# First mixture of a two-layer decoder: token weights multiplied into the up product's operand by GpSimd, eight experts' results summed in one bank

## The chip, the cores and the metric

The kernel is one program on one core of a Trainium2 chip. The time is device time in microseconds, the median of several runs. A core has TensorE (PE: matrix products, with PEld for its weight loads), VectorE (DVE), ScalarE (ACT), GpSimd (POOL) and the queue engine SyncE (SP), which here only issues transfers. Each engine works through its own instructions in order; they wait for each other by semaphores.

## The reference

Four batches of 512 tokens of 128 features go through two layers of self attention, cross attention and a mixture of experts. Only the first mixture, on 2048 tokens with 8 experts, matters here:

```python
hidden = x.reshape(-1, H)
routing_weights = jax.nn.softmax(hidden @ gate_w.T, axis=-1)
topk_weights, topk_indices = jax.lax.top_k(routing_weights, 2)
topk_weights = topk_weights / (jnp.sum(topk_weights, axis=-1, keepdims=True) + EPS)
...
routed = routed / (jnp.sum(routed, axis=-1, keepdims=True) + EPS)
...
gate_up = jnp.einsum('th,ehq->teq', hidden, gate_up_proj)
gate, up = jnp.split(gate_up, 2, axis=-1)
expert_outputs = jnp.einsum('teq,eqh->teh', jax.nn.silu(gate) * up, down_proj)
out = jnp.sum(expert_outputs * routed[:, :, None], axis=1)
```

`x` in this formula is the layer norm of the residual rows, and `out` is added to them. `routed` holds a token's weight for each expert, zero for six of eight.

## The kernel before

The first stage of the program (`stage_front`) holds the first layer. Its end, 400 to 510 us of the trace, is the mixture, written as 32 turns: turn `t` is expert `t % 8` of batch `t // 8`. The order of the work on each engine is written out by hand: a loop over `t` on each engine, in which `if t == ...` lines put the rest of the work (what is left of cross attention, layer norms, routing, the layer norm `lq` for the next stage) between the turns.

All experts are computed for all tokens. In a turn TensorE does `gate_up(t)`: a gate and an up product of a whole batch, 512 tokens, into a bank each (L553, L554). Then it does `down_of(t - 1)`, the down product of the turn before, as four products of 128 tokens (L568). ScalarE takes the gate through SiLU (L1009, `silu_of`). VectorE multiplies that by the up result (L836, `hidden`). Both products of `gate_up` read the transposed, normalized rows of the batch in `g.XT`. The down result of each expert lies in one of two banks, tokens on the partitions. VectorE multiplies it by the tokens' weights and adds it to the residual rows `g.X` in four instructions, one for each 128 tokens (L847, `add(t - 1)`, at the end of the turn after):

```python
for i in range(SB):
    n = SB * b + i
    x = g.X[:, n, :]
    last = dve.scalar_tensor_tensor(out=x, in0=down[k][:, i, :], scalar=rt.route[:, e, n:n + 1],
                                    in1=x, op0=ALU.mult, op1=ALU.add)
```

The routing of a batch runs through these steps: TensorE's `route_of` (L545), then on VectorE `rt.shift`, with ScalarE an exponential (L1248), on VectorE `rt.softmax`, `rt.first`, `rt.second` and `rt.weigh`, some 25 short instructions (L1253 to L1290) of which each waits for the one before. The last raises `rt.done`. The rows for it come from a layer norm: `ln2` has statistics on VectorE (L115, L118), the inverse root on GpSimd (L124, L126), the normalization on VectorE (L132), transposes on TensorE (`rows_turn2`, of `ln` `rows_turn`, L159) and a copy on ScalarE (L166). `ln` and `lq` have the same steps. `cross_of`, `cross_add` (L775), `y_of`, `residual` (L749), `logits_of` and `soften` belong to attention and cross attention of batches 2 and 3, which end inside the mixture. `last_pair_head` and `last_pair_tail` (L822 on) are the last heads of the self attention.

## Time and profile before

| | us |
|---|---|
| median of 3 runs | 1030.67 |
| lowest and highest run | 1028.32, 1035.21 |
| profiled execution, first to last instruction (span) | 1028.4 |
| TensorE busy in it | 925.0 |
| VectorE busy in it | 761.6 |
| ScalarE busy in it | 624.5 |
| GpSimd busy in it | 510.8 |

The profiled execution's own time is its span; the page gives no other. Busy times are sums of instruction times; TensorE's instructions overlap in its pipeline, so what one of them costs is read from the start of it to the start of the next. All rows below name lines of the kernel before. A 32-bit product appears as two instructions in the trace.

### The profile page before, as it was taken

Reading aid. Unit: us, or ns where it says so; the run is one execution under the profiler, and the core shown is the slowest. Engines: PE = TensorE matmul, PEld = TensorE weight load, DVE = VectorE, ACT = ScalarE, POOL = GpSimd, SP = SyncE. Lnnn points to the kernel's source line nnn. Section 1 sums busy time; section 2 is a strip of 40 time slices with the busy share of each in tenths; the row PEclk is TensorE's granted clock in tenths of the full one; section 3 lists DMA queues with packets and bytes.
Section 4 is the critical chain, followed back from the end, with each engine's and each line's share of the span. In section 5 each row is a group of like instructions: output and inputs, shape, how many; then the busy total and the mean of one; then the engine's idle time right before and its main releaser. Section 6 shows DMA issues by size and latency. Waiting matters only on the chain. (4 is left out here: it accounts for less than half of the span.)

```text
span 1028.4 us, 20270 instructions
## 1 busy us (share of the span) xinstructions
PE 925.0 (90%) x6146; PEld 480.8 (47%) x6146; DVE 761.6 (74%) x1656; ACT 624.5 (61%) x1500; POOL 510.8 (50%) x847
## 2 busy tenths in 40 slices
PE   3999999999999997899889999999999997888296
PEld 1222222222332334565455555555555564567296
DVE  7799899889999976889745666666656665676464
ACT  4388888888888883233266665665566652354164
POOL 6366666776554462100144454455445443775544
PEclk8599999999999999999999999999999997696599
DMA  4099920000000000000060000000000000000240
GB/s 103 1 237 245 245 60 1 2 1 2 2 1 0 0 1 1 1 1 1 8 206 6 15 9 7 8 13 5 8 5 13 0 2 1 0 2 16 89 122 19
DMA packets 50684, 37.49 MB, mean 36 GB/s; under 512 B 15737, under 2 KB 48677, under 8 KB 50608
## 3 DMA queue, kind: packets, MB, share of 16 engines
q1 hardware_dynamic: 48864, 32.83, 13.4%
q0 software_dynamic: 1744, 3.72, 1.1%
q8 instruction: 39, 0.64, 0.3%
q14 instruction: 37, 0.30, 0.1%
HBM read 15.54 MB, written 21.45 MB: 36 GB/s over the span
## 5 line engine op out<-in xcount | busy, mean ns | idle before, releaser
L725 DVE TENSOR_REDUCE a_nmax<-a_rows 128x2 f32<-128x1024 f32 x256 | 299.7, 1218 | 26.5 <-PE a_rows L439 23.6
L979 ACT ACTIVATE a_probs<-a_turned 128x512 f32<-128x512 f32 x512 | 270.0, 605 | 48.2 <-PE a_turned L465 46.9
L1451 POOL TENSOR_TENSOR a_prob<-a_prob,a_rinv 128x256 f32<-128x256 f32 (+3 forms) x128 | 159.4, 1253 | 163.9 <-DVE a_rinv L1647 163.6
L1640 DVE TENSOR_REDUCE a_nmax<-a_score 128x2 f32<-128x256 f32 (+3 forms) x128 | 105.6, 825 | 116.5 <-PE a_score L1497 112.2
L1594 ACT ACTIVATE a_prob<-a_score,a_nmax 128x128 f32<-128x128 f32 (+3 forms) x256 | 132.6, 523 | 81.9 <-DVE a_nmax L1640 81.3
L465 PE MATMUL a_turned<-a_q,a_qk 32*128 32x512 bf16 x512 | 136.9, 389 | 7.3 <-ACT a_probs L979 4.9
L424 PE MATMUL a_acc<-a_probs,a_vg 128*32 128x512 f32 x1024 | 138.1, 611 | 0.2
L439 PE MATMUL a_rows<-a_qk 32*128 32x512 bf16 x512 | 108.9, 398 | 5.9 <-DVE a_nmax L725 3.9
L465 PEld LDWEIGHTS a_turned<-a_q,a_qk 32*128 32x128 bf16 x512 | 34.9, 91 | 153.8 <-ACT a_probs L979 125.8
L1494 PE MATMUL a_score<-a_k_s,a_q_s 64*128 64x384 f32 (+3 forms) x512 | 103.7, 481 | 2.2 <-ACT a_prob L1594 1.3
L1653 DVE COPY a_pt<-a_turn 128x128 f32<-128x128 f32 (+3 forms) x224 | 92.2, 447 | 1.4 <-PE a_turn L1508 1.4
L1508 PE MATMUL a_turn<-g_ident,a_prob 128*128 128x128 f32 x640 | 91.8, 274 | 1.0 <-POOL a_prob L1451 0.6
L1521 PE MATMUL a_acc<-a_pt,a_v_s 128*64 128x256 f32 (+3 forms) x512 | 76.0, 439 | 0.8 <-ACT a_pt L1601 0.8
L1508 PEld LDWEIGHTS a_turn<-g_ident,a_prob 128*128 128x128 f32 x640 | 67.9, 141 | 1.7 <-POOL a_prob L1451 1.4
L1521 PEld LDWEIGHTS a_acc<-a_pt,a_v_s 128*64 128x64 f32 x512 | 34.2, 136 | 49.2 <-issue 43.3
L1494 PEld LDWEIGHTS a_score<-a_k_s,a_q_s 64*128 64x128 f32 x512 | 38.6, 184 | 37.5 <-issue 17.8
L1594 ACT ACTIVATION_READ_ACCUMULATOR a_prob<-a_score,a_nmax 128x1 f32 x256 | 50.2, 196 | 0.0
L1601 ACT ACTIVATE a_pt<-a_turn 128x512 f32<-128x512 f32 x32 | 19.1, 597 | 46.6 <-PE a_turn L1508 46.6
L2103 ACT ACTIVATE c_hid<-c_turn,c_b1s 128x128 f32<-128x128 f32 x92 | 26.2, 368 | 34.1 <-PE c_turn L2001 34.1
L568 PEld LDWEIGHTS a_rows<-a_wdn,a_probs 128*128 128x128 f32 x256 | 32.9, 191 | 26.6 <-issue 14.8
L1191 POOL TENSOR_TENSOR a_rms<-a_ms,g_mhalf 128x16 f32<-128x16 f32 x15 | 43.7, 2913 | 1.2
L1140 POOL TENSOR_TENSOR a_qs<-a_nmax,a_none 128x16 bf16<-128x16 f32 x32 | 8.4, 263 | 72.0 <-DVE a_nmax L725 71.8
(351 smaller groups left out, 1580.7 us busy)
## 6 DMA issues: line engine op xcount, KB each, us to landing
xs_sorted<-a_blank SPq DMA_DIRECT2D x9, 1935.0 KB
m_m_w<-L_ffn_w SPq DMA_DIRECT2D x8, 512.0 KB, 9.2
c_xs<-xs_sorted SPq DMA_DIRECT2D x23, 129.0 KB, 2.1
g_a_wq<-L_attn_Wq SPq DMA_DIRECT2D x32, 64.0 KB, 2.1
g_X<-x SPq DMA_DIRECT2D x4, 256.0 KB, 4.7
a_wgu<-L_ffn_gate_up_proj SPq DMA_DIRECT2D x1, 1024.0 KB, 5.5
a_wdn<-L_ffn_down_proj SPq DMA_DIRECT2D x1, 512.0 KB, 6.8
g_a_wk<-L_attn_Wk SPq DMA_DIRECT2D x8, 64.0 KB, 1.9
```

Source lines behind the costliest of these rows:

```text
L424: last = pe.matmul(acc[32 * j:32 * j + 32, :], vg[i % 2][:, tb, j // 2, :], probs[:, (tb % 2) * 4 + j, :], start=(tb == 0 and i % 2 == 0), ...
L439: last = pe.matmul(rows[n % 2][:, jj, :], qk[i % 3][q, 0, sb * P:(sb + 1) * P], qk[i % 3][q, 1, :], start=True, stop=True)
L465: pe.matmul(turned[n % 3][:, :], qk[(i - 1) % 3][q, 1, tb * P:(tb + 1) * P], q2[(i - 1) % 2][q, :], start=True, stop=True).then_inc(turn_i ...
L725: dve.tensor_reduce(nmax[i % 2][:, p // 2, (p % 2) * 2:(p % 2) * 2 + 2], rows[n % 2][:, :, :], AX_X, ALU.max, negate=True).then_inc(row_ou ...
L979: act.activation(probs[:, (tb % 2) * 4 + j, :], turned[n % 3][:, :], ACT.Exp, scale=float(HD0) ** -0.5).then_inc(turn_out, 1)
L1451: pool.tensor_tensor(pr, pr, spread(rinv[:, t % RING, :], 2, width), ALU.mult).then_inc(scl, 1)
L1494: pe.matmul(score[t % 2][:, j, 0:width], q_s[i % 2][p][h, sb * P:(sb + 1) * P], k_s[i // 2 % 2][h, 0:width], start=True, stop=False)
L1508: last = pe.transpose(turn[j][:, tb * P:(tb + 1) * P], prob[t % RING][:, j, tb * P:(tb + 1) * P], g.ident[:, :])
L1521: last = pe.matmul(acc[j * HD1:(j + 1) * HD1, tb * P:S], v_s[i // 2 % 2][:, j, tb, :], pt[p][j][:, tb, tb * P:S], start=(tb == 0), stop=(t ...
L1594: act.activation(prob[t % RING][:, j, 0:width], score[t % 2][:, j, 0:width], ACT.Exp, bias=nmax[:, t % RING, j:j + 1], accum_out=rsum[:, t ...
L1640: dve.tensor_reduce(nmax[:, t % RING, :], score[t % 2][:, :, 0:width], AX_X, ALU.max, negate=True).then_inc(mx, 1)
L1653: dve.tensor_copy(pt[p][j][:, 0:sb + 1, sb * P:(sb + 1) * P], turn[j][:, 0:(sb + 1) * P].rearrange("p (a s) -> p a s", s=P)).then_inc(copi ...
```

## The change

Batch 0 stays as it is. For batches 1 to 3 the token weight is no longer applied to the down result. The weights of a batch, tokens on the partitions, are transposed by TensorE to one row of 512 tokens for each expert (`share_turn`), copied by ScalarE to 8 partitions of SBUF (`share_copy`) and written to memory by SP's queue (16 KB). From there they are read back in four transfers of 512 KB, two experts each, in which the same rows go to all 128 partitions. GpSimd multiplies the batch's transposed rows by an expert's weight row (`route_rows`), two turns ahead, into one of three buffers, and the up product of that turn reads this buffer. Gate, SiLU and hidden product stay. The hidden values of all eight experts are then already weighted, and their down products add up in one bank, without a read between. VectorE adds that bank to the residual rows once a batch (`add_batch`). Around that the order of the other work is changed on all engines: attention and cross attention of batches 2 and 3 and the routing of batches 1 to 3 come earlier. The buffers are those of the self attention, which is over by then.

```diff
-        part = [probs[:, 4 + i, :].rearrange("p (t d) -> p t d", d=D) for i in range(2)]
+        routed = [probs[:, 4 + i, :] for i in range(3)]
+        share = g.q_tok[:, :, :, :].rearrange("p i t w -> p (i t w)").bitcast(F32).rearrange(
+            "p (n e s) -> p n e s", n=2, e=E)
+        share_rows = o_sb[0:E, :]
+        share_d = nc.dram_tensor("route_rows", (B, E, S), F32).ap()
...
             sp.wait_ge(blank_d, 16 * (SLOTS1 // BLANK))
+            for b in range(1, B):
+                sp.wait_ge(share_copied, b)
+                sp.dma_start(share_d[b], share_rows).then_inc(share_out, 16)
+                sp.wait_ge(share_out, 16 * b)
+                wait(sp, s_xr, E * (b - 2))
+                for e in range(0, E, 2):
+                    sp.dma_start(share[:, b % 2, e:e + 2, :], share_d[b, e:e + 2].partition_broadcast(P)
+                                 ).then_inc(share_in[b, e], 16)
...
-                pe.matmul(up[k][:, :], wgu[:, e, D:2 * D], g.XT[:, b * S:(b + 1) * S], start=True, stop=True).then_inc(s_u, 1)
+                if b:
+                    pe.wait_ge(s_xr, t - E + 1)
+                rows_of = routed[t % 3] if b else g.XT[:, 0:S]
+                pe.matmul(up[k][:, :], wgu[:, e, D:2 * D], rows_of, start=True, stop=True).then_inc(s_u, 1)
...
+                if b == 0:
+                    wait(pe, s_dx, t - 1)
+                elif e == 0:
+                    pe.wait_ge(s_dx, (E - 1, E, E + 1)[b - 1])
                 for i in range(SB):
-                    last = pe.matmul(down[k][:, i, :], hid[k][:, i * P:(i + 1) * P], wdn[:, e, :], start=True, stop=True)
+                    last = pe.matmul(down[k][:, i, :], hid[t % 2][:, i * P:(i + 1) * P], wdn[:, e, :],
+                                     start=(b == 0 or e == i == 0), stop=(b == 0 or e == E - 1), skip_group_check=b > 0)
...
+            def share_turn(b):
+                pe.wait_ge(rt.done, b + 1)
+                if b == 1:
+                    pe.wait_ge(s_x, 3)
+                for t in range(SB):
+                    last = pe.transpose(share_bank[b][0:E, t * P:(t + 1) * P], rt.route[:, :, SB * b + t], g.ident[:, :])
+                last.then_inc(share_turned, 1)
...
+                if t == 6:
+                    share_turn(1)
...
+                if t == 13:
+                    share_turn(2)
...
+                if t == 21:
+                    share_turn(3)
...
+            def add_batch(b):
+                dve.wait_ge(s_dn, E * (b + 1))
+                x = g.X[:, SB * b:SB * b + SB, :]
+                dve.tensor_tensor(x, x, down[(b + 1) % 2], ALU.add).then_inc(s_dx, 1)
...
+            def share_copy(b):
+                act.wait_ge(share_turned, b)
+                wait(act, share_out, 16 * (b - 1))
+                act.activation(share_rows, share_bank[b][0:E, :], ACT.Copy).then_inc(share_copied, 1)
...
+            def route_rows(t):
+                b, e = t // E, t % E
+                if e == 0:
+                    ln2.ready(pool, b)
+                pool.wait_ge(share_in[b, e // 2 * 2], 16)
+                wait(pool, s_u, t - 2 if t >= E + 3 else 0)
+                pool.tensor_tensor(routed[t % 3], g.XT[:, b * S:(b + 1) * S], share[:, b % 2, e, :], ALU.mult
+                                   ).then_inc(s_xr, 1)
```

On VectorE the moved work stands as follows. Cross attention's sum for batch 2 (`cross_sum`) goes from turn 4 to turn 2, its addition and statistics from 7 to 3, the end of the last pair from 7 to 4. The routing of batch 1 goes from turns 4, 5 and 6 to 3, 4 and 5, the layer norm `ln2` of batch 2 from 9 to 5, the residual addition of batch 3 from 8 to 6 and the layer norm `ln` of batch 3 from 10 to 7. The second pick and the weights of batches 2 and 3 go from turns 16 and 24 to 12 and 20.

TensorE around the start of batch 1, before: gate and up product of turn 7 (into `turned2`, `turned0`), down product of turn 6, gate and up product of turn 8, the first of batch 1 (into `acc`, `turned1`).

```order
L553 MATMUL a0_turned2<-g_XT,a0_wgu 128x512
L554 MATMUL a0_turned0<-g_XT,a0_wgu 128x512
L568 MATMUL a0_rows1<-a0_wdn,a0_probs 128x128 x4
L553 MATMUL a0_acc<-g_XT,a0_wgu 128x512
L554 MATMUL a0_turned1<-g_XT,a0_wgu 128x512
```

The same place after; `a0_route` are the token weights, and in the last row `a0_probs` is the buffer of `route_rows`.

```order
L598 MATMUL a0_rows0<-g_ident,a0_route 8x128 x4
L570 MATMUL a0_turned2<-g_XT,a0_wgu 128x512
L574 MATMUL a0_turned0<-g_XT,a0_wgu 128x512
L589 MATMUL a0_rows1<-a0_wdn,a0_probs 128x128 x4
L159 MATMUL a0_rows0<-g_ident,g_XN 128x128 x4
L570 MATMUL a0_acc<-g_XT,a0_wgu 128x512
L574 MATMUL a0_turned1<-a0_probs,a0_wgu 128x512
```

Two sets of transposes moved between these products, the first of which waits for batch 1's routing, and the up product of turn 8 now reads what GpSimd wrote and waits for it, ahead of the down product of turn 7.

GpSimd in the same turns, before: the root of the last pair (L1217), the layer norm `ln2` of batch 2, then `ln` of batch 3 and `lq` of batch 0.

```order
L1217 TENSOR_TENSOR a0_rms<-a0_ms,g_mhalf 128x16 [waits a0_last_squares]
L124 TENSOR_SCALAR a0_ln2_ve<-a0_ln2_mv 128x4 [waits a0_ln2_aggr]
L126 TENSOR_TENSOR a0_ln2_rstd<-a0_ln2_ve,g_mhalf 128x4 [waits a0_ln2_eps]
L124 TENSOR_SCALAR a0_ln_ve<-a0_ln_mv 128x4 [waits a0_ln_aggr]
L126 TENSOR_TENSOR a0_ln_rstd<-a0_ln_ve,g_mhalf 128x4 [waits a0_ln_eps]
L124 TENSOR_SCALAR a0_lq_ve<-a0_lq_mv 128x4 [waits a0_lq_aggr]
```

And after; `share_in10` counts the transfer of batch 1's experts 0 and 1, `share_in12` that of 2 and 3.

```order
L1259 TENSOR_TENSOR a0_rms<-a0_ms,g_mhalf 128x16 [waits a0_last_squares]
L124 TENSOR_SCALAR a0_ln2_ve<-a0_ln2_mv 128x4 [waits a0_ln2_aggr]
L126 TENSOR_TENSOR a0_ln2_rstd<-a0_ln2_ve,g_mhalf 128x4 [waits a0_ln2_eps]
L1249 TENSOR_TENSOR a0_probs<-g_XT,u_q_tok 128x512 [waits a0_share_in10,a0_ln2_xt]
L124 TENSOR_SCALAR a0_ln_ve<-a0_ln_mv 128x4 [waits a0_ln_aggr]
L126 TENSOR_TENSOR a0_ln_rstd<-a0_ln_ve,g_mhalf 128x4 [waits a0_ln_eps]
L1249 TENSOR_TENSOR a0_probs<-g_XT,u_q_tok 128x512 [waits a0_share_in10]
L1249 TENSOR_TENSOR a0_probs<-g_XT,u_q_tok 128x512 [waits a0_share_in12]
```

The layer norm `ln` of batch 3 now stands behind the first product, which waits for a transfer.

## Rows read from the trace of the kernel before

**Rows 1.** Turns 0-8, 9-31: length, busy PE, PEld, DVE, ACT, POOL; clock, DMA share, GB/s.

```profile
400.00:434.70 34.70, 29.06 (x131) 18.27 (x132) 26.96 (x115) 10.65 (x17) 4.16 (x3) 0.95 0.00 1
434.70:509.00 74.30, 69.07 (x337) 44.40 (x335) 65.95 (x258) 23.38 (x37) 7.59 (x12) 1.00 0.00 1
```

**Rows 2.** Waits, 399 to 511 us: us in total, times, longest.

```profile
PEld a_rows L568 <- DVE a_probs L836: 11.6, 7, 2.4
```

**Rows 3.** TensorE in order of time: start, us, line, out<-in, instructions.

```profile
417.52 0.96 PE L545 MATMUL a_rows<-g_gwt,g_XT 128*128 128x8 f32 x8
...
434.71 1.02 PE L553 MATMUL a_turned<-g_XT,a_wgu 128*128 128x512 f32 x2
...
474.95 0.60 PE L159 MATMUL a_rows<-g_ident,g_XN 128*128 128x128 f32 x4
475.39 1.02 PE L553 MATMUL a_turned<-g_XT,a_wgu 128*128 128x512 f32 x2
476.25 1.02 PE L554 MATMUL a_turned<-g_XT,a_wgu 128*128 128x512 f32 x2
...
478.00 0.96 PE L545 MATMUL a_rows<-g_gwt,g_XT 128*128 128x8 f32 x8
478.81 1.11 PE L553 MATMUL a_acc<-g_XT,a_wgu 128*128 128x512 f32 x2
...
506.81 2.16 PE L568 MATMUL a_rows<-a_wdn,a_probs 128*128 128x128 f32 x16
```

**Rows 4.** Groups of instructions, 399 to 511 us: the weighted additions.

```profile
L847 DVE SCALAR_TENSOR_TENSOR g_X<-a_rows,a_route,g_X 128x128 f32<-128x128 f32 x128 | 35.7, 341 | 0.8 <-issue 0.3
```

**Rows 5.** VectorE in order of time.

```profile
424.22 0.18 DVE L1259 TENSOR_REDUCE a_rt_v<-a_rt_p 128x4 f32<-128x32 f32 x1
...
427.63 0.18 DVE L1276 SCALAR_TENSOR_TENSOR a_rt_pick<-a_rt_pick,a_rt_p 128x32 f32<-128x32 f32 x1
...
431.03 1.12 DVE L847 SCALAR_TENSOR_TENSOR g_X<-a_rows,a_route,g_X 128x128 f32<-128x128 f32 x4
...
432.66 0.28 DVE L822 TENSOR_TENSOR a_both<-a_both,a_rms 128x128 f32<-128x128 f32 x1
...
435.48 1.09 DVE L847 SCALAR_TENSOR_TENSOR g_X<-a_rows,a_route,g_X 128x128 f32<-128x128 f32 x4
...
441.49 1.12 DVE L847 SCALAR_TENSOR_TENSOR g_X<-a_rows,a_route,g_X 128x128 f32<-128x128 f32 x4
442.53 0.67 DVE L836 TENSOR_TENSOR a_probs<-a_probs,a_turned 128x512 f32<-128x512 f32 x1
443.12 1.11 DVE L132 TENSOR_SCALAR g_XN<-g_X,a_ln_mv,a_ln_rstd 128x128 f32<-128x128 f32 x4
```

**Rows 6.** Groups of GpSimd's instructions, whole span.

```profile
L1830 POOL TENSOR_TENSOR c_wg<-c_w,g_c_gp 128x512 f32<-128x512 f32 x16 | 20.3, 1270 | 1.3 <-ACT c_w L2065 1.2
...
L126 POOL TENSOR_TENSOR a_ln_rstd<-a_ln_ve,g_mhalf 128x4 f32<-128x4 f32 x9 | 9.3, 1037 | 0.8
...
L124 POOL TENSOR_SCALAR a_ln_ve<-a_ln_mv 128x4 f32<-128x4 f32 x9 | 2.1, 230 | 51.6 <-DVE a_ln_mv L118 51.6
```

**Rows 7.** Groups of instructions, 399 to 511 us: ScalarE's copies of a bank.

```profile
L166 ACT ACTIVATE g_XT<-a_rows 128x512 f32<-128x512 f32 x8 | 4.8, 597 | 16.6 <-PE a_rows L159 16.6
```

**Rows 8.** Transfers: number, KB each, median us from issue to landing.

```profile
m_m_w<-L_ffn_w SPq DMA_DIRECT2D x8, 512.0 KB, 9.2
...
a_wgu<-L_ffn_gate_up_proj SPq DMA_DIRECT2D x1, 1024.0 KB, 5.5
...
g_a_wk<-L_attn_Wk SPq DMA_DIRECT2D x8, 64.0 KB, 1.9
...
out<-c_ysb,c_token POOLq DMA_INDIRECT x23, 2.6
```

**Rows 9.** Two stretches of batch 0, columns as in the first group.

```profile
412.00:414.00 2.00, 0.95 (x5) 0.98 (x6) 2.00 (x9) 0.00 (x0) 0.00 (x0) 0.62 0.00 0
414.00:416.00 2.00, 2.00 (x4) 0.93 (x4) 1.86 (x6) 0.71 (x2) 0.00 (x0) 0.52 0.00 0
```

More of the change, by code:

```diff
@@ L283, in stage_front @@
         silu, hid = [probs[:, i, :] for i in range(2)], [probs[:, 2 + i, :] for i in range(2)]
[L284 to L288 removed]
+        routed = [probs[:, 4 + i, :] for i in range(3)]
[3 more added lines that the diff above has]
+        share_d = nc.dram_tensor("route_rows", (B, E, S), F32).ap()
+        share_bank = {1: quarter[1], 2: quarter[1], 3: quarter[0]}
+        blank = sc.sb("blank", [P, 1, ROW1])
+        m0_in, s_g, s_u, s_si, s_h, s_dn, s_dx, blank_s, blank_d = (
+            sc.sem(n) for n in ("expert_weights_in", "gate", "up", "silu", "hidden", "down", "down_residual", "blank_set",
+                                "slots_blank"))
+        share_turned, share_copied, share_out, s_xr = (
+            sc.sem(n) for n in ("share_turned", "share_copied", "share_out", "routed_rows"))
+        share_in = {(b, e): sc.sem(f"share_in{b}{e}") for b in range(1, B) for e in range(0, E, 2)}
         (lastc, last_ms, last_rt, last_done, nw_in, nws, used, laid, zero, diag_in, mask_in, s_bias, s_y, s_res, s_lg, s_l1, s_nm, s_z, s_e, s_sum, s_r, s_w, s_wt,
@@ L871, in _ @@
                 if t == 2:
+                    cross_sum(2)
                     last_pair_head()
+                if t == 3:
+                    rt.shift(dve, route_link, 1, SB, 2 * SB, route_logits(own[1], SB))
+                    cross_add(2)
+                    stats2(2)
                 if t == 4:
-                    rt.shift(dve, route_link, 1, SB, 2 * SB, route_logits(own[1], SB))
-                    cross_sum(2)
-                if t == 5:
                     rt.softmax(dve, route_link, 1, SB, 2 * SB)
@@ L904, in _ @@
                     cross_add(3)
                     stats2(3)
+                if t == 15:
+                    ln2.vector_norm(dve, (3,))
+                if t == 17:
+                    add_batch(1)
+                if t == 18:
+                    rt.shift(dve, route_link, 3, 3 * SB, NT, route_logits(own[3], SB))
                 if t == 19:
-                    ln2.vector_norm(dve, (3,))
-                if t == 21:
-                    rt.shift(dve, route_link, 3, 3 * SB, NT, route_logits(own[3], SB))
@@ L1009, in silu_of @@
                 act.activation(silu[k], gate[k][:, :], ACT.Silu).then_inc(s_si, 1)
-            def scale_down(t):
-                b, e, k = t // E, t % E, t % 2
-                if e == 0:
-                    act.wait_ge(rt.done, b + 1)
-                act.wait_ge(s_dn, t + 1)
-                wait(act, s_ad, t - 1)
-                for i in range(SB):
-                    n = SB * b + i
-                    last = act.activation(part[k][:, i, :], down[k][:, i, :], ACT.Copy, scale=rt.route[:, e, n:n + 1])
-                last.then_inc(s_cp, 1)
+            def share_copy(b):
+                act.wait_ge(share_turned, b)
+                wait(act, share_out, 16 * (b - 1))
+                act.activation(share_rows, share_bank[b][0:E, :], ACT.Copy).then_inc(share_copied, 1)
             run(act, body)
```

145 lines of the change are left out of this document (66 added, 79 removed).

## The prediction

> **What bounds the kernel now.** The change lies in one stretch of the program, the first mixture: 32 turns (4 batches of 8 experts) between 400.0 and 509.0 us. I read the busy times of that stretch first, cut at the start of turn 9 [rows 1]. From turn 9 on TensorE is busy 69.1 of 74.3 us and VectorE 66.0: TensorE is the limit there, VectorE is close behind it. Before that, TensorE is busy 29.1 of 34.7 us. The waits say for whom it stood: its weight loads for the down product stood 11.6 us for VectorE's hidden product [rows 2]. Those stalls are what a lighter VectorE can give back.
>
> TensorE's rows in order of time give its floor [rows 3]. Where nothing stalls, a gate product takes 0.86 us from its start to the next one's (475.39 to 476.25), and gate, up and down together 2.61 (475.39 to 478.00), so down takes 0.89. A batch's transposes into a bank take 0.44 (474.95 to 475.39), a routing product 0.81 (478.00 to 478.81). From the gate of turn 9 (434.71) to the end of the last down product (506.81 + 2.16 = 508.97) are 74.3 us. The work in it is 23 turns of 2.61, one more down of 0.89 and what is inserted: six sets of a batch's transposes (0.44 each), two routing products and one of cross attention's logits, of as many instructions (0.81 each), one single transpose (a quarter of 0.44) and a 128x512 product (0.86). That is 60.9 + 6.0 = 66.9, so at most some 7 us can be gained behind turn 9. The whole stretch's idle TensorE time is 34.7 + 74.3 - 29.1 - 69.1 = 10.8 us by [rows 1], and half of it lies ahead of turn 9, nearly all in batch 0, which keeps its old additions.
>
> **The change part by part.** *Additions.* Of the 128 weighted additions (0.28 us each from start to start, 35.7 us in all [rows 4]) 96 go, and three of 0.67 us (the price of a 128x512 VectorE instruction, [rows 5] at 442.53) come. VectorE loses 25 us, nearly all behind turn 9; there it falls from 66 busy us to about 41 of some 70. Worth on the path: the stalls behind turn 9, no more. TensorE's own work from the gate of turn 9 on becomes 66.2: one batch's transposes, one routing product and the layer norm's transposes leave for turns 7 and 8 (1.7), and two batches' share transposes enter (4 small transposes, priced as a batch's, 0.44 each). **Credit: 74.3 - 66.2 = 8.1 us.**
>
> *Products on GpSimd.* 24 products of 128x512 f32 with two operands. The nearest row is the same shape in a later stage, 1270 ns, 16 times [rows 6]. A turn is 2.61, so GpSimd keeps up; only the first product of each batch can be late.
>
> *The way of the token weights.* This is what has no row of its own. From the end of routing (weights ready on VectorE) to the first up product: 4 transposes (0.44), the copy on ScalarE (0.60, the price of its 128x512 copies [rows 7]), a write of 16 KB to memory, a read of the first pair of experts (512 KB), the product (1.27), and five hand-overs of about 0.1. The write: a 64 KB read lands 1.9 us after its issue, the only small writes 2.6 [rows 8]; I take 2.1, nearer to the first since both go out from SP's queue. The read: 64 KB lands in 1.9 and 1024 KB in 5.5; interpolated by size, 512 KB land in 3.6. The bounds are these two rows; eight such transfers issued together took 9.2 in the median, which is the rival below. Sum: 0.44 + 0.60 + 2.1 + 3.6 + 1.27 + 0.5 = **8.5 us**, with 6.6 and 10.9 from the rows' ends (write 1.9 or 2.6, read 1.9 or 5.5). The Trainium skill (DMA: Bandwidth & Descriptors, Anatomy of one DMA) gives 2.0 us plus the bytes at 436 GB/s, for another kind of queue; by it the write and the read would take 2.0 and 3.2, an estimate, and the prediction would be 1.5 us lower. No row here shows a broadcast read of this size.
>
> *Batch 0 becomes longer.* VectorE is the limit there, and work is moved into it. Route logits of batch 1 stand where they stood, ready at 417.52 + 0.96 = 418.5 [rows 3]. Behind them VectorE now does, from [rows 5]: the shift (two of the short steps of which 16 take 3.40, so 0.4), cross attention's addition, its statistics and the end of the last pair (2.82, 432.66 to 435.48), an addition (1.04, 441.49 to 442.53) and a hidden product (0.59, 442.53 to 443.12), then softmax, both picks, the weights with an addition and a hidden product between them (6.81, 424.22 to 431.03). Batch 1's weights are ready at 418.5 + 0.4 + 2.82 + 1.04 + 0.59 + 6.81 = 430.2. The first up product of batch 1 can start 8.5 later, at 438.7. TensorE is there earlier: VectorE goes on with a layer norm (1.1, at 443.12), an addition and the hidden product of turn 6 (with its end 0.7), until 433.0; then down (0.89), transposes (0.44) and gate (0.86): 435.2. It **stalls 3.5 us**, with the down product of turn 7 and all that follows queued behind the waiting up product. GpSimd stands in the same wait, and the layer norm of batch 3's rows is queued behind its product: 438.6 + 0.23 + 1.04 + 0.1 = 440.0 [rows 6], VectorE's part 1.1, ready at 441.1. TensorE needs them after up, down and routing at 438.7 + 0.86 + 0.89 + 0.81 = 441.3, so this second wait is just covered; if the product is 0.3 us slower than I take it nothing changes, since both shift. With the transposes (0.44) the gate of turn 9 starts at 441.7, where it was 434.7. **Debit: 7.0.**
>
> *Batches 2 and 3.* The share transposes stand two gate-up-down rounds and one gate ahead of the up product that needs them: 5.22 + 0.86 = 6.1 us, in batch 3 plus a layer norm's transposes, 6.5. What is left of the way behind the transposes is 8.0. **Stalls: 1.9 and 1.5.** The transposes also wait for the weights: hidden (0.59) and second pick with weights (3.40, 427.63 to 431.03), 4.0 and a hand-over after the up product, where TensorE needs 0.86 + 0.89 + 1.72 + 0.89 = 4.4 in batch 2 and 3.5 in batch 3. In batch 2 the VectorE starts about a microsecond late, since two changes of ScalarE's table (for the exponentials, as now) hold up the turn before. I take 0.7 and 0.6.
>
> *End.* One addition of 0.67 in place of four that take 1.04: -0.4.
>
> *Clock.* In batch 0, with TensorE waiting (busy 0.95 of 2 us), the granted clock fell to its lower level of 1.2 GHz, a mean of 0.62 in one stretch of 2 us and 0.52 in the next [rows 9]. That cost 2 x 0.38 + 2 x 0.48 = 1.7 us of work. Ahead of the first up product of batch 1 TensorE will be just as idle, 4.4 us of work (transposes twice, gate and up, down, gate) between the last down product at about 429 and 438.7. I expect one such fall more at that price; the bounds are 0 and two of them, 3.4.
>
> Sum: -8.1 + 7.0 + 1.9 + 1.5 + 0.7 + 0.6 - 0.4 + 1.7 = **+4.9 us**. The span of the profiled execution is 1028.4 us, 2.3 under the median of 1030.67 and equal to the fastest run. Set on the median: **1035.6 us**.
>
> **The rivals.** *The weights come in time.* With write and read at 1.9 us each the way is 6.6; of the stalls 1.9 + 1.9 + 1.5 go, and the fall of the clock with them (1.7): 4.9 - 7.0 = -2.1, **1028.6 us**. For it: 64 KB land in 1.9, and a broadcast read asks memory for few different bytes. Against it: the destination still takes 512 KB.
>
> *The four reads land together.* If the 2 MB share the engines instead of following one another, the first pair lands with the last. Eight reads of 512 KB took 9.2 us in the median [rows 8], 5.6 over my price; three batches give 16.8, **1052 us**. Against it: those eight stood in a queue with others and the median is the fourth's. It decides from 2 us over my price: then 1035.6 + 3 x 1.9 is over 1041, slower by more than 1%.
>
> *GpSimd's products hold up VectorE.* Of the 16 instructions of second pick and weights, eight read two tensors from SBUF, as the product does. If such an instruction can't start while a product runs, the 3.40 us meet one or two products: 1.3 to 2.5 us later weights in batches 2 and 3, +2.6 to +5.0, **1039.4 us** in the middle. The trace before has no GpSimd product beside such a chain. The Trainium skill (SBUF — State Buffer, SBUF: two separate sides) calls the port pair that the two engines share an exclusive lock, which a VectorE instruction with two SBUF inputs and a GpSimd instruction hold for their whole length; by that rule this rival is the forecast, and no row here shows it.
>
> *A gain of over 1%* would need all 10.8 idle us of the stretch and no stall for the weights.
>
> **How the numbers follow.** Forecast 0.52, early weights 0.22, held-up VectorE 0.12, reads together 0.10, a gain over 1% 0.04. Differences under 1% (1020 to 1041 us) are about what a measurement of this kernel can't tell from none. The range, 1027 to 1046, takes in the early weights, the forecast with the way at 10.9 (+2.4 in each of three batches, 1042.8) and the held-up VectorE with a second fall of the clock; it leaves out most of the reads together. Slower by over 1%: the reads together (0.10), a third of the held-up VectorE (0.04) and the forecast's end beyond 2 us more on the way (0.04), 0.18. Faster by over 1%: 0.04. Within: 0.78.
>
> **What would show it.** In the profile after: the first up product of each later batch waits for GpSimd, and GpSimd for a transfer, some 3.5, 1.9 and 1.5 us; no stall of TensorE for VectorE behind turn 9 but at the share transposes; the gate of turn 9 near 441.7 from the same start; VectorE busy about 25 us less. I am wrong if the read lands in under 2 us or over 6, if VectorE's chain of 3.40 grows beside the products, or if batch 0 doesn't get longer.

## The result, and the profile after

The changed kernel takes 1045.28 us in the median, against 1030.49 for the kernel before. Executions more than 1.5% over a kernel's fastest are left out of the ratios and of the last column of the table below: here one of four, of 2794.39 us (the median without it is 1043.37), further down one of e2 and two of e9, all three near 1048. The ratio is 1.0131, 95% interval 1.0092 to 1.0170, some 13 us. The forecast was 1035.6 with a range of 1027 to 1046. The profiled execution took 1042.28 us; its span is 1040.7 where it was 1028.4, so 12.3 us are to be found.

The stretch of the mixture holds 11.2 of them. TensorE in order of time, the columns as in [rows 3]; L570 is the gate product, L574 up, L589 down, L598 the transposes of the token weights, L159 transposes of a layer norm's rows. Behind an arrow stands what ended the idle time before the instruction.

```profile
399.53 1.10 PE L570 MATMUL a_acc<-g_XT,a_wgu 128*128 128x512 f32 x2 [0.78 <-ACT g_XT L166]
...
429.44 0.60 PE L598 MATMUL a_rows<-g_ident,a_route 128*8 128x128 f32 x4 [0.96 <-DVE a_route L1330]
...
433.51 1.02 PE L570 MATMUL a_acc<-g_XT,a_wgu 128*128 128x512 f32 x2
437.60 1.13 PE L574 MATMUL a_turned<-a_probs,a_wgu 128*128 128x512 f32 x2 [3.07 <-POOL a_probs L1249]
...
443.03 1.08 PE L159 MATMUL a_rows<-g_ident,g_XN 128*128 128x128 f32 x4 [1.48 <-DVE g_XN L132]
443.91 1.91 PE L570 MATMUL a_turned<-g_XT,a_wgu 128*128 128x512 f32 x2
...
461.69 0.60 PE L598 MATMUL a_rows<-g_ident,a_route 128*8 128x128 f32 x4 [1.74 <-DVE a_route L1330]
...
469.64 1.12 PE L574 MATMUL a_turned<-a_probs,a_wgu 128*128 128x512 f32 x2 [1.26 <-POOL a_probs L1249]
...
476.07 0.63 PE L159 MATMUL a_rows<-g_ident,g_XN 128*128 128x128 f32 x4 [0.57 <-DVE g_XN L132]
...
489.30 0.60 PE L598 MATMUL a_rows<-g_ident,a_route 128*8 128x128 f32 x4 [2.16 <-DVE a_route L1330]
...
517.50 2.16 PE L589 MATMUL a_rows<-a_wdn,a_probs 128*128 128x128 f32 x16
```

From the gate of turn 0 (399.53) to the gate of turn 9 (443.91) are 44.4 us, where it was 34.7 [rows 1]: 9.7 lost. From there to the end of the last down product (519.66) are 75.75, where it was 74.3: the credit of 8.1 is gone too. The arrows name where TensorE stood: two waits around the first up product of batch 1 (3.07 for GpSimd, 1.48 for a layer norm on VectorE), two at the transposes of the weights (1.74 and 2.16, for VectorE's routing), 1.26 at the first up product of batch 2, 0.57 for another layer norm.

The same two stretches by engine, columns as in [rows 1], and two short ones inside them:

```profile
399.50:443.90 44.40, 32.42 (x151) 21.02 (x152) 35.39 (x143) 11.72 (x19) 11.60 (x11) 0.95 0.13 48
443.90:519.70 75.80, 70.02 (x329) 44.91 (x327) 43.99 (x141) 23.96 (x38) 30.02 (x28) 0.96 0.16 57
...
439.00:445.80 6.80, 5.32 (x21) 4.22 (x20) 6.55 (x13) 0.60 (x1) 3.55 (x3) 0.50 0.03 11
490.20:493.60 3.40, 3.40 (x9) 1.85 (x8) 1.32 (x9) 0.92 (x2) 1.26 (x2) 0.50 0.18 63
```

VectorE is no longer near its limit behind turn 9 (44.0 of 75.8 us busy, it was 66.0 of 74.3). The two short stretches stood at the lower clock, 1.2 GHz (granted 0.50). In the second TensorE was busy throughout, so it cost half of 3.4, 1.7 us; the first began between the two waits around turn 8 and reached 1.9 us behind the gate of turn 9.

VectorE and GpSimd, in order of time, show where the layer norm's wait is from. L132 writes the normed rows, four instructions a batch; L1249 is the product; L1307 and L1309 are two steps of a pick, L1316 begins the second pick, and L872 is the hidden product. The first two rows, of SP's queue, are the write of batch 1's weights and the issue of the four reads:

```profile
430.75 0.32 SPq L420 DMA_DIRECT2D route_rows<-a_o_sb  x1
432.26 1.77 SPq L424 DMA_DIRECT2D u_q_tok<-route_rows  x4
```

```profile
436.29 1.26 POOL L1249 TENSOR_TENSOR a_probs<-g_XT,u_q_tok 128x512 f32<-128x512 f32 x1 [14.48 <-DMA u_q_tok<-route_rows]
437.51 0.23 POOL L124 TENSOR_SCALAR a_ln_ve<-a_ln_mv 128x4 f32<-128x4 f32 x1
437.82 1.04 POOL L126 TENSOR_TENSOR a_ln_rstd<-a_ln_ve,g_mhalf 128x4 f32<-128x4 f32 x1
438.83 3.71 POOL L1249 TENSOR_TENSOR a_probs<-g_XT,u_q_tok 128x512 f32<-128x512 f32 x3
...
470.88 4.96 POOL L1249 TENSOR_TENSOR a_probs<-g_XT,u_q_tok 128x512 f32<-128x512 f32 x4
```

```profile
438.90 3.98 DVE L132 TENSOR_SCALAR g_XN<-g_X,a_ln_mv,a_ln_rstd 128x128 f32<-128x128 f32 x4 [3.49 <-POOL a_ln_rstd L126]
...
455.89 1.17 DVE L1307 TENSOR_TENSOR a_rt_t<-a_rt_t,g_rank 128x32 f32<-128x32 f32 x1
...
458.14 0.18 DVE L1316 SCALAR_TENSOR_TENSOR a_rt_pick<-a_rt_pick,a_rt_p 128x32 f32<-128x32 f32 x1
...
458.81 0.19 DVE L1307 TENSOR_TENSOR a_rt_t<-a_rt_t,g_rank 128x32 f32<-128x32 f32 x1
...
461.54 0.69 DVE L872 TENSOR_TENSOR a_probs<-a_probs,a_turned 128x512 f32<-128x512 f32 x1
...
471.21 0.69 DVE L872 TENSOR_TENSOR a_probs<-a_probs,a_turned 128x512 f32<-128x512 f32 x1 [2.77 <-issue]
471.82 4.10 DVE L132 TENSOR_SCALAR g_XN<-g_X,a_lq_mv,a_lq_rstd 128x128 f32<-128x128 f32 x4
...
483.88 1.22 DVE L1309 TENSOR_TENSOR a_rt_pick<-a_rt_t,a_rt_v 128x32 f32<-128x32 f32 x1
```

The norm that took 1.11 us before [rows 5] takes 3.98: its first instructions end one at a time with GpSimd's three products (438.83 + 3.71 = 442.54). In batches 2 and 3 one step of the first pick takes 1.2; the same step takes 0.19 in the second pick (458.81). The 16 instructions of second pick and weights, from 458.14 to 461.54, take 3.40 as before [rows 5]: no product ran beside them. No semaphore makes the long instructions wait for the products; they run long beside them.

### The profile page after: what moved, and what is told of

The parts are those of the page before. It is cut to its first block and busy times, and to the rows that moved or that the text cites. A ratio compares the mean times of both kernels' runs of the same rounds, so it can differ in the third digit from the quotient of the medians.

```text
span 1040.7 us, 20227 instructions
## 1 busy us (share of the span) xinstructions
PE 929.2 (89%) x6158; PEld 484.3 (47%) x6158; DVE 747.2 (72%) x1563; ACT 626.5 (60%) x1503; POOL 540.9 (52%) x871
## 5 line engine op out<-in xcount | busy, mean ns | idle before, releaser
L761 DVE TENSOR_REDUCE a_nmax<-a_rows 128x2 f32<-128x1024 f32 x256 | 299.7, 1218 | 26.2 <-PE a_rows L454 23.4
L1634 ACT ACTIVATE a_prob<-a_score,a_nmax 128x128 f32<-128x128 f32 (+3 forms) x256 | 132.8, 523 | 80.8 <-DVE a_nmax L1680 80.2
L1249 POOL TENSOR_TENSOR a_probs<-g_XT,u_q_tok 128x512 f32<-128x512 f32 x24 | 30.0, 1268 | 35.5 <-PE a_turned L574 19.2
```

The lines of the kernel that those rows point to most:

```text
L761: dve.tensor_reduce(nmax[i % 2][:, p // 2, (p % 2) * 2:(p % 2) * 2 + 2], rows[n % 2][:, :, :], AX_X, ALU.max, negate=True).then_inc(row_ou ...
L1634: act.activation(prob[t % RING][:, j, 0:width], score[t % 2][:, j, 0:width], ACT.Exp, bias=nmax[:, t % RING, j:j + 1], accum_out=rsum[:, t ...
```

## The experiments

One table for all. "Gate 9" is the time from the gate of turn 0 to the gate of turn 9, "behind" from there to the end of the last down product, both from the one profiled execution; the median is of all timed executions, the ratio to the kernel before on the same chip. The last column is the mean time of an execution at the lower clock, worked out from its span and mean granted clock: (1 - clock) x 2 x span, since the granted clock has two levels in these traces, 1.0 and 0.5 of full speed.

| kernel | gate 9 | behind | sum | median | ratio (95%) | at half clock |
|---|---|---|---|---|---|---|
| before | 34.7 | 74.3 | 109.0 | 1030.4 to 1032.9 | 1 | 122.7 to 124.0 |
| changed | 44.4 | 75.75 | 120.1 | 1045.28 | 1.0131 (1.0092 to 1.0170) | 132.8 |
| e1 no weights | 39.8 | 66.8 | 106.6 | 1034.32 | 1.0029 (1.0003 to 1.0056) | 138.6 |
| e2 small powers | 41.65 | 72.1 | 113.7 | 1038.74 | 1.0049 (1.0015 to 1.0082) | 120.4 |
| e3 norm first | 41.35 | 74.4 | 115.8 | 1041.75 | 1.0127 (1.0074 to 1.0180) | 127.0 |
| e4 on VectorE | 41.7 | 72.8 | 114.5 | 1040.87 | 1.0108 (1.0074 to 1.0142) | 122.9 |
| e5 no weights in batch 1 | 39.5 | 74.4 | 113.95 | 1036.44 | 1.0049 (1.0021 to 1.0077) | 128.0 |
| e6 early down | 44.7 | 76.1 | 120.8 | 1044.23 | 1.0116 (1.0056 to 1.0177) | 130.4 |
| e7 combined | 39.9 | 72.2 | 112.2 | 1032.99 | 1.0006 (0.9976 to 1.0037) | 116.6 |
| e8 combined, on VectorE | 40.6 | 71.5 | 112.1 | 1036.17 | 1.0047 (1.0013 to 1.0081) | 123.8 |
| e9 order pair | 40.4 | 73.6 | 113.95 | 1035.28 | 1.0026 (0.9995 to 1.0057) | 117.6 |
| e10 turn earlier | 43.4 | 76.1 | 119.5 | 1045.29 | 1.0113 (1.0059 to 1.0168) | 131.0 |
| e11 changed, again | 45.0 | 76.3 | 121.3 | 1046.24 | 1.0130 (1.0079 to 1.0181) | 134.4 |

Line numbers in the rows below are those of each run's own kernel.

My theory: the loss is the way of the weights to the first up product of each batch, and GpSimd's products that hold up VectorE. The rival: the loss is batch 0's longer order, in which other work was moved ahead, and the long instructions on VectorE cost nothing.

**e1, neither weights nor products.**

```diff
-                if b:
-                    pe.wait_ge(s_xr, t - E + 1)
-                rows_of = routed[t % 3] if b else g.XT[:, 0:S]
+                rows_of = g.XT[:, b * S:(b + 1) * S]
...
-                if t == 6:
-                    share_turn(1)
...
-                if E <= t + 2 < T:
-                    route_rows(t + 2)
```

> Weights and products left out: batches 1 to 3 sum their experts unweighted in one bank, no transposes of the weights, no write or reads, no products; the order of the other work is that of the changed kernel. If the loss lies in the way of the weights and in GpSimd's products, TensorE stalls nowhere for them: the gate of turn 9 comes some 37 to 38 us after the gate of turn 0 (44.4 in the changed kernel, 34.7 before), from there to the end of the last down product it takes its own work, 65.3 us (75.8), and the whole is about 1025 us, some 5 under the kernel before. If the loss lies in batch 0's longer order and the other work's new places, it stays at 1036 or more.

In the trace the theory holds behind turn 9 and half ahead of it:

```profile
401.00 2.05 PE L560 MATMUL a_acc<-g_XT,a_wgu 128*128 128x512 f32 x2 [0.78 <-ACT g_XT L166]
...
440.80 1.02 PE L560 MATMUL a_turned<-g_XT,a_wgu 128*128 128x512 f32 x2
...
505.44 2.16 PE L577 MATMUL a_rows<-a_wdn,a_probs 128*128 128x128 f32 x16
```

Behind turn 9 it takes 66.8 us (440.80 to 507.60): the credit is real, 7.5 us, where nothing waits for weights. But the gate of turn 9 still comes 39.8 after that of turn 0, 5 us later than before, and 2 over what I expected; part is clock, since the first gate itself ran at the lower one (2.05 us for 1.10). And the time did not follow: 1034 instead of 1025. Between 380 us and the gate of turn 9 this execution shows three stretches at half clock, of which the first ends before the mixture begins:

```profile
387.00:394.00 7.00, 7.00 (x28) 3.44 (x31) 3.22 (x14) 1.01 (x3) 0.99 (x4) 0.51 0.00 0
400.70:404.10 3.40, 3.10 (x4) 1.51 (x5) 1.73 (x11) 0.47 (x2) 1.27 (x2) 0.51 0.00 0
428.00:431.40 3.40, 3.40 (x11) 2.36 (x11) 3.02 (x15) 0.10 (x1) 0.00 (x0) 0.52 0.01 2
```

The profiled execution tells where the gain went: its span is 1031.1 us, 2.7 over the kernel before's, though its mixture is 2.4 us shorter. The first gate starts 1.0 later (401.00 for 400.01), and from the end of the last down product to the end of the program it takes 523.5 where it was 519.4; nothing that this kernel leaves out lies there. Its ten executions stood at half clock for 138.6 us in the mean, the kernel before for 123.5. What such a microsecond goes with can be read from the kernel before alone: over the 20 executions measured beside e1 the time rises by 0.48 us for each more at half clock. By that slope, an estimate, the 15 us more are worth some 7. Why this kernel spends more time there stays open.

**e2, the hold alone.** GpSimd keeps its waits and almost its time, but touches only a few numbers.

```diff
-                pool.tensor_tensor(routed[t % 3], g.XT[:, b * S:(b + 1) * S], share[:, b % 2, e, :], ALU.mult
+                pool.tensor_tensor(routed[t % 3][:, 0:5], ms[:, 0:5], g.mhalf[:, 0:5], ALU.pow
                                    ).then_inc(s_xr, 1)
...
-                rows_of = routed[t % 3] if b else g.XT[:, 0:S]
+                rows_of = g.XT[:, b * S:(b + 1) * S]
```

> Each product is replaced by a power of 128x5 numbers on GpSimd (estimated at 1.2 us, nearly as long as a product), with every wait and transfer kept; the up product reads the unweighted rows, so the result is unweighted. If GpSimd's products hold up VectorE's instructions that only touch SBUF, the layer norm of 3.98 us falls to 1.1, the two routing instructions of 1.17 and 1.22 us to 0.19, the waits behind turn 9 shrink by some 1.5 + 0.7 + 1.0 + 1.0, and the time is 1036 to 1038 us. If those instructions were long for another reason, or their length costs nothing, it stays at 1042.

GpSimd and VectorE at the place where the norm took 3.98, then TensorE at the two transposes of weights behind turn 9:

```profile
441.63 3.43 POOL L1249 TENSOR_TENSOR a_probs<-a_ms,g_mhalf 128x5 f32<-128x5 f32 x3
```

```profile
441.69 1.12 DVE L132 TENSOR_SCALAR g_XN<-g_X,a_ln_mv,a_ln_rstd 128x128 f32<-128x128 f32 x4 [3.41 <-POOL a_ln_rstd L126]
```

```profile
459.36 0.60 PE L598 MATMUL a_rows<-g_ident,a_route 128*8 128x128 f32 x4 [0.76 <-DVE a_route L1330]
...
485.61 0.60 PE L598 MATMUL a_rows<-g_ident,a_route 128*8 128x128 f32 x4 [1.13 <-DVE a_route L1330]
```

GpSimd is as busy beside the norm as before (three instructions, 3.43 us), and the norm takes 1.12: all four of its instructions are done before the first power is. The waits at the transposes fall from 1.74 and 2.16 to 0.76 and 1.13, by 1.0 each, the length of the one routing step that was held. VectorE's busy time over the span falls from 747.2 to 738.2 us; the excess of the five long groups in the changed kernel (2.9 + 3.0 + 0.8 for the norms, 1.0 twice) is 8.7. So the hold is real, and it belongs to the product and not to GpSimd's being busy, nor to the transfers, which stay in e2; whether its operands or its operation make it, e2 does not separate, since it changes both. And it is on the path: 72.1 us behind turn 9, and 1038.74 in all, a little over the 1036 to 1038 expected; the interval of the ratio ends at 1.0082, the changed kernel's begins at 1.0092 (in e11 at 1.0079). Part of that gain can be clock (120.4 us at the lower one for 132.8).

**e3, the layer norm ahead of the first product.** On GpSimd only:

```diff
+                if t == 6:
+                    ln.gpsimd(pool, (3,))
                 if E <= t + 2 < T:
                     route_rows(t + 2)
...
-                if t == 6:
-                    ln.gpsimd(pool, (3,))
```

> GpSimd's part of the layer norm of batch 3's rows stands ahead of its first product. If the layer norm was late because of the products that ran beside it, it now runs before them in 1.1 us, TensorE's 1.5 us wait ahead of the gate of turn 9 goes, and with it some of the half clock: 1039 to 1041 us. If the order on GpSimd makes no difference: 1042.

TensorE around turn 8:

```profile
400.18 1.10 PE L570 MATMUL a_acc<-g_XT,a_wgu 128*128 128x512 f32 x2 [0.78 <-ACT g_XT L166]
...
438.39 1.12 PE L574 MATMUL a_turned<-a_probs,a_wgu 128*128 128x512 f32 x2 [3.20 <-POOL a_probs L1249]
...
441.53 1.02 PE L570 MATMUL a_turned<-g_XT,a_wgu 128*128 128x512 f32 x2
```

The norm's wait ahead of the gate of turn 9 is gone and the gate comes at 41.35, within 0.4 of what the prediction had (441.7 from 400.0). The time hardly moved: 1041.75, ratio 1.0127, an interval too wide to tell it from the changed kernel. The trace shows the mechanism, the time does not show a gain.

**e4, products on VectorE.** The same function called on VectorE, two turns ahead of the turn that needs the product, the first of a batch one turn ahead.

```diff
+                dve.tensor_tensor(routed[t % 3], g.XT[:, b * S:(b + 1) * S], share[:, b % 2, e, :], ALU.mult
+                                   ).then_inc(s_xr, 1)
...
+                if t + 1 >= E and (t + 1) % E == 0 and t + 1 < T:
+                    route_rows(t + 1)
+                if t + 2 > E and (t + 2) % E and t + 2 < T:
+                    route_rows(t + 2)
```

> The 24 products are made by VectorE (some 0.6 us each) in place of GpSimd. No holding up, but 14.4 us more work on VectorE. If the holding costs more than VectorE's own time: 1037 to 1041 us. If VectorE's load is what counts: 1045 or more.

No norm or routing step is long in its trace, the stretch is 114.5 us, 1.3 under e3, and the time 1040.87. VectorE has 24 more instructions of 0.68; the interval is too wide to say that it is a better or a worse place for them than GpSimd.

**e5, batch 1 without weights**, batches 2 and 3 as in the changed kernel.

```diff
-                if b:
-                    pe.wait_ge(s_xr, t - E + 1)
-                rows_of = routed[t % 3] if b else g.XT[:, 0:S]
+                if b > 1:
+                    pe.wait_ge(s_xr, t - 2 * E + 1)
+                rows_of = routed[t % 3] if b > 1 else g.XT[:, b * S:(b + 1) * S]
...
-                if E <= t + 2 < T:
+                if 2 * E <= t + 2 < T:
                     route_rows(t + 2)
```

> Weights, their way and the products are left out in batch 1 alone; batches 2 and 3 stand as in the changed kernel. If batch 1's way is the larger part of the loss, the gate of turn 9 comes 37 to 38 us after that of turn 0 (44.4 in the changed kernel, 41.3 with the norm moved), and the time is 4 to 7 us under the changed kernel's, a ratio to before of 1.006 to 1.009. If batches 2 and 3 carry the loss, the ratio stays at 1.011 or more. Behind turn 9 the stalls at the transposes of the weights of batches 2 and 3 (1.9 and 2.3 us) stay in both cases.

1036.44 us, a ratio of 1.0049: with batch 1's weights and products more than half of the loss goes, by the ratio and by the stretch (6.2 of 11.2 us). The gate of turn 9 comes at 39.5, though, as in e1: of the 9.7 us lost there, 4.9 go with batch 1's weights and products and 4.8 stay. Those belong to batch 0's order (in this execution with 3.4 us of it at half clock, as many as the kernel before has in batch 0). The rival has half of batch 0 right. The transposes of the weights of batches 2 and 3, of which I expected both waits to stay:

```profile
453.19 0.60 PE L594 MATMUL a_rows<-g_ident,a_route 128*8 128x128 f32 x4 [0.75 <-DVE a_route L1322]
...
481.42 0.60 PE L594 MATMUL a_rows<-g_ident,a_route 128*8 128x128 f32 x4 [2.15 <-DVE a_route L1322]
```

Batch 2's wait falls to 0.75, as in e2: its routing has no products beside it now, since those were batch 1's. Batch 3's, whose routing still has batch 2's products beside it, stays at 2.15. That confirms the hold a second time, without a change to the products that are left.

**e6, the down product first.** At turns 8, 16 and 24 the down product of the turn before is issued ahead of the up product that waits.

```diff
+                if b and e == 0:
+                    down_of(t - 1)
                 if b:
                     pe.wait_ge(s_xr, t - E + 1)
...
-                if t:
+                if t % E:
                     down_of(t - 1)
```

> At the start of batches 1 to 3 the down product of the turn before stands ahead of the up product that waits for GpSimd. If that product waits for the weights while ready work stands behind it, 0.9 us of each wait are covered: the wait ahead of the first up product of batch 1 falls from 3.1 to some 2.2 us, in batch 2 from 1.4 to 0.5, together 1.8 to 2.6 us, 1040 to 1043 us. If TensorE waits for VectorE behind it anyhow, the hidden product of the turn comes no earlier and the time stays at 1042 to 1045.

TensorE around turn 8:

```profile
438.15 1.13 PE L576 MATMUL a_turned<-a_probs,a_wgu 128*128 128x512 f32 x2 [1.29 <-POOL a_probs L1251]
...
443.57 1.08 PE L159 MATMUL a_rows<-g_ident,g_XN 128*128 128x128 f32 x4 [3.51 <-DVE g_XN L132]
444.46 1.91 PE L570 MATMUL a_turned<-g_XT,a_wgu 128*128 128x512 f32 x2
```

The wait for the weights falls from 3.07 to 1.29, and the wait for the held norm behind it grows from 1.48 to 3.51. Nothing is gained: 1044.23 us.

**e9, both of these together** (and batch 2's routing product ahead of the same wait).

```diff
+                if b and e == 0:
+                    down_of(t - 1)
+                if t == E:
+                    route_of(2, (2,), own[2])
...
+                if t == 6:
+                    ln.gpsimd(pool, (3,))
                 if E <= t + 2 < T:
                     route_rows(t + 2)
```

> Two of the combined kernel's four edits: GpSimd's part of the layer norm ahead of its first product, and the down product (at batch 1 the routing product too) ahead of the up product that waits. Each alone gave nothing that could be measured. If each only uncovered the other's wait, both together bring the gate of turn 9 to 40 to 40.5 us after that of turn 0 (41.3 with the norm alone, 44.7 with the early down alone) and the stretch to 113.5 to 114.5 us, a ratio to before of 1.005 to 1.009. If they do nothing together either, 1.011 or more.

```profile
442.51 1.12 PE L578 MATMUL a_turned<-a_probs,a_wgu 128*128 128x512 f32 x2 [0.52 <-POOL a_probs L1252]
443.48 0.60 PE L159 MATMUL a_rows<-g_ident,g_XN 128*128 128x128 f32 x4
443.91 1.02 PE L570 MATMUL a_turned<-g_XT,a_wgu 128*128 128x512 f32 x2
```

Of the two waits 0.52 us is left. e6's edit, which only uncovered the norm's wait, pays beside e3's: the gate of turn 9 comes at 40.4, 1.0 earlier than in e3. The ratio is 1.0026, against 1.0127 and 1.0116 for either alone, but that gain (1%, some 10 us) is not shown to be the edits': the stretch is only 1.8 us shorter than in e3, whose ratio rests on four executions from 1038.08 to 1048.64 us, and e9's stand 117.6 us at half clock, those of e3 127.0 and of e6 130.4.

**e10, routing of batches 2 and 3 a turn earlier**, with e3's edit; the transposes of the weights stay in their turns.

```diff
-                if t == 11:
+                if t == 10:
                     rt.softmax(dve, route_link, 2, 2 * SB, 3 * SB)
                     rt.first(dve, route_link, 2 * SB, 3 * SB)
-                if t == 12:
+                if t == 11:
                     rt.second(dve, route_link, 2 * SB, 3 * SB)
                     rt.weigh(dve, route_link, 2 * SB, 3 * SB, 1e-9)
...
-                if t == 10:
+                if t == 9:
                     rt.scalar(act, 2, 2 * SB, 3 * SB)
                     cross_exp(3)
```

> Two other edits of the combined kernel: the norm's part first, and the routing of batches 2 and 3 a turn earlier on VectorE and ScalarE, the transposes of the weights left in their places. If the weights' lateness in batches 2 and 3 is the larger part of what was given back, the waits at the transposes (1.9 and 2.3 us) go, the up products' own waits of 1 to 2 us stay, the stretch takes 112 to 113.5 us and the ratio is 1.003 to 1.007. If the waits only move from the transposes to the up products or to the hidden products, 115 or more and 1.010 or more.

The waits at both transposes are gone, and the time is the changed kernel's, 1045.29, as the second of the two expectations had it. TensorE's waits over the stretch, us in total, times, longest:

```profile
PE a_rows L589 <- DVE a_probs L873: 5.9, 6, 1.9
PE a_turned L574 <- POOL a_probs L1250: 5.2, 3, 3.4
```

The down products now wait 5.9 us for VectorE's hidden products (2.9 in e3), behind which the routing has moved. The gate of turn 9 came late in this execution because the clock fell there, as it did in the changed kernel, though the norm was in time:

```profile
439.00:445.90 6.90, 6.90 (x25) 5.29 (x24) 1.81 (x5) 1.59 (x3) 2.58 (x3) 0.51 0.10 40
```

**e7, all of it,** with expert 0's weights read alone ahead of the pairs.

```diff
-                for e in range(0, E, 2):
-                    sp.dma_start(share[:, b % 2, e:e + 2, :], share_d[b, e:e + 2].partition_broadcast(P)
+                for e, n in ((0, 1), (1, 1), (2, 2), (4, 2), (6, 2)):
+                    sp.dma_start(share[:, b % 2, e:e + n, :], share_d[b, e:e + n].partition_broadcast(P)
                                  ).then_inc(share_in[b, e], 16)
```

> Four edits together: GpSimd's part of the layer norm ahead of its first product, the early down product (with batch 2's routing product behind it, also ahead of the wait), expert 0's weights read alone ahead of the pairs, and the routing of batches 2 and 3 on VectorE and ScalarE a turn earlier, with the transposes of the weights left where they were. If the stalls found in the trace are what the change loses, the waits at the transposes (1.9 and 2.3 us) go, those of the first up products fall under 1 us in batches 2 and 3, and from the gate of turn 0 to the last down product it takes 108 to 111 us (120.1 in the changed kernel, 109.0 before): no slower than before within 0.4%. If other stalls take their place, 114 or more and a ratio over 1.006.

```profile
401.79 1.10 PE L570 MATMUL a_acc<-g_XT,a_wgu 128*128 128x512 f32 x2 [0.78 <-ACT g_XT L166]
...
441.71 1.02 PE L570 MATMUL a_turned<-g_XT,a_wgu 128*128 128x512 f32 x2
...
511.79 2.16 PE L593 MATMUL a_rows<-a_wdn,a_probs 128*128 128x128 f32 x16
```

No up product waits a microsecond, no transpose of batches 2 and 3 waits. The ratio is 1.0006, no different from the kernel before; the stretch, 112.2 us, is a little over what I expected and 3.2 over the kernel before's, so part of the equal time can be clock (116.6 us at the lower one for 122.7). What is left of the loss is batch 0 (39.9 where it was 34.7), and behind turn 9 down products that wait 2.9 us in all for VectorE (of 5.8 in the whole stretch).

**e8, the same with the products on VectorE.**

```diff
-                if E <= t + 2 < T:
-                    route_rows(t + 2)
...
+                if t + 2 > E and (t + 2) % E and t + 2 < T:
+                    route_rows(t + 2)
```

> The same with the products on VectorE in place of GpSimd. If the holding up is still worth more than 14 us of VectorE's otherwise idle time, 107 to 110 us for the same stretch and 1 to 2 us under the combined kernel with GpSimd; if not, 1 to 3 us over it.

The stretch is the same (112.1), the ratio 1.0047; the intervals of e7 and e8 overlap, so neither engine is shown better.

**e11, the changed kernel once more.**

> The changed kernel once more, on the same chip as the two others. If the time at half clock differs from execution to execution by where the clock's stretches fall, the profile shows other stretches at half clock than the first one did, the same waits at the same places, and a ratio of 1.010 to 1.014. If the fall of the clock at the gate of turn 9 belongs to the wait there, it is there again.

A ratio of 1.0130, as the first time, and the same waits: 3.14 for the first product, 2.62 for the norm, 1.75 and 2.15 at the transposes. Two stretches of this execution, columns as in [rows 1]:

```profile
445.50:448.90 3.40, 2.89 (x7) 1.89 (x8) 3.03 (x11) 0.66 (x2) 0.03 (x1) 0.51 0.00 0
...
493.20:496.70 3.50, 3.50 (x8) 1.44 (x6) 1.22 (x9) 1.18 (x2) 1.26 (x2) 0.52 0.09 15
```

The clock fell beside the same two places as the first time, around the gate of turn 9 (446.89) and behind batch 3's transposes, but at the first of them only from 445.6 us, at the end of the norm's wait, and once more in batch 0 (414.9 to 418.3), where it had not. So the waits belong to the kernel, and the falls shift around them from one execution to the next.

## Why the prediction was right, and where it was off

The forecast was slower by 4.9 us and it was slower by some 13: right in sign, within the range near its upper end (e11's median of 1046.24 lies just over it), about a third of the size. That it lies within is partly luck: the upper part of the range stood for a slower way of the weights or for a chain of second pick and weights that grows with a second fall of the clock, and neither the way nor that chain was longer. What filled it was a hold of other VectorE instructions and a longer batch 0; the outcome is the one that the prediction gave 0.18, slower by over 1%. Step by step:

- *Credit, 8.1.* Right as TensorE's own work: e1 needs 66.8 us behind turn 9, 1.5 more than that work comes to without the two sets of transposes of the weights (66.2 - 0.9). In the changed kernel it is eaten by the stalls below.
- *The way of the weights, 8.5 us.* Right, with two sizes off that cancel: from the transposes (429.44) to the first up product (437.60) it took 8.2, in which the write took 1.5 us to the issue of the reads (430.75 to 432.26) for 2.1, and the first read 4.0 to its product for 3.6 and a hand-over. The up product came 38.1 us after the gate of turn 0 where 38.7 was expected. The stall was 3.07 for 3.5. The rivals of weights in time and of reads that land together are both out: the first read was there after 4 us (issue at 432.26, product at 436.29), the median of the twelve after 5.7.
- *"This second wait is just covered".* This step failed. The norm queued behind the product was not 1.1 us but 3.98, since GpSimd's next three products ran beside it; TensorE waited 1.48 and 2.62 us in two executions. I had named the mechanism for the chain of second pick and weights alone and given it 0.12, and had not looked at what else VectorE does while GpSimd works off its first products. That chain, which I had named as a sign of being wrong, did not grow: it took 3.40 as before.
- *Debit, 7.0.* Mis-sized: 9.7 us by the trace, 4.9 for batch 1's weights and products, 4.8 for the order of batch 0 (e1, e5), where the working had 3.5 for each.
- *Transposes of the weights in batches 2 and 3, 0.7 and 0.6.* Mis-sized: 1.74 and 2.16. One microsecond of each is a held step of the first pick. Without it (e2) they are 0.76, as forecast, and 1.13, where VectorE comes half a microsecond later than I had it.
- *Stalls 1.9 and 1.5 at the first up products of batches 2 and 3.* 1.26 and none. The second was covered by the fall of the clock at 490.2: e3, without that fall, has 1.47 and 0.87 there, e11, with one, 1.75 and none.
- *VectorE 25 us less busy.* 14.4 (761.6 to 747.2): the hold took 8.7 of the rest. In e2, without it, 23.4.
- *Clock, 1.7.* Mis-sized. In the mixture the profiled execution stands 10.2 us at half clock, and e11's as many, where the kernel before stood 3.4. Over the whole program the executions of the changed kernel stand 132.8 and 134.4 us there (measured twice), those of the kernel before 123 to 124: some 10 us more, by the slope of 0.48 about 5 of the 13, an estimate.

The third rival is what came true beside the forecast: GpSimd's products hold up VectorE. The Trainium skill (SBUF — State Buffer, SBUF: two separate sides) says that VectorE's instructions in a mode that takes two ports, or with two inputs from SBUF, and GpSimd's exclude one another for a whole instruction. The trace agrees for what was held: the norm, which goes from SBUF to SBUF, and routing steps with two SBUF inputs, each until the product's end; the hidden product, which reads one input from PSUM, ran beside products in its usual 0.67 to 0.69 (471.21, beside the products from 470.88). In e2 the trace does not agree that GpSimd's whole instruction counts: the norm ran to its end within a power of 128x5, which also reads SBUF.

The theory's rival has a part of it: half of the debit ahead of turn 9 is work moved into batch 0, where VectorE was already the limit, and e7, which removes nearly every stall that the change itself made, ends level with the kernel before and not under it. What stays open is the clock: why kernels with nearly the same instructions differ by 9 to 14 us at half clock (e7 and e9 against e3, e6, e10), and why e1 has the most. In the profiles the fall at 439 to 449 us is in the changed kernel twice, in e6 and in e10, and in none of e2, e3, e4, e7, e9; e3 and e4 had the wait of over 3 us too, so the wait alone does not decide it. Most of the time at half clock lies where no edit reaches: in the profiled executions 27 to 38 us in the first 70 us of the program and 72 to 87 behind 850 us. From the end of the last down product to the end of the program they take 517.0 us (e4, 74.7 at half clock behind 850) to 523.5 (e1, 86.9). Differences of that size between kernels are not shown to come from the mixture.

## What to carry to other kernels

When work like these products is moved to GpSimd, list everything that VectorE does from SBUF to SBUF while the new instructions run, above all in the burst after a wait, when several run back to back; its own queue behind the first instruction belongs to that list. A path of transposes, copy, write, broadcast read and product costs 8 us from weights to first use here, so a consumer that has less than that much ready work ahead of it stalls, and the work behind its wait should be issued ahead of it. Of two waits in a row one can hide behind the other, as in e6: try the edits together before dropping either.

## What the hardware showed that was not expected

A GpSimd product of 128x512 holds a 0.3 us VectorE instruction until its own end, 1.29 us each over three of them, but a GpSimd power of 128x5 of nearly the same length (1.17 us, also from SBUF to SBUF) holds nothing: the norm's four instructions ran in 1.12 us, all within one of them (e2). So it is not the length of GpSimd's instruction that counts; whether it is its operands or its operation stays open.

Time at half clock differs between executions of one kernel by enough to move it 1%: the kernel before ran from 1027.9 to 1041.1 us on one chip, at a mean granted clock of 0.944 and 0.932. A difference of one profile's stretch to another's is not the difference of two kernels' times.
